# New order tables for an attention and mixture-of-experts kernel: queries before keys in the first batch, and a planner with other durations and tiling prices

## The reference

```python
n = layernorm(x)
q, k, v = split(n @ W_attn.T)                      # 16 heads of 8 channels
K, V = sums of k, v over the blocks of 4, 8, ..., 1024 tokens       # 511 "sets"
logits = concat(q @ K.T / sqrt(8), masked to sets that ended;  q . K_tail)   # tail: own, unfinished block
att = softmax(logits);  out = att @ V + att_tail * V_tail
x = x + out @ W_proj.T
h = layernorm(x); scores = sigmoid(h @ gate_w.T) + e_bias
combine = weights of the 6 best of 32 experts, within the 4 best of 8 groups
x = x + sum_e combine[e] * relu(h @ up[e].T)**2 @ down[e] + relu(h @ shared_up.T)**2 @ shared_down
```

## Time and profile before

| | |
|---|---|
| time, median of 3 runs | 617.42 us (615.31 to 617.7) |
| profiled execution | span 616.0 us; no other time is listed for it |
| TensorE busy | 556.2 us, 90% of the span |
| VectorE busy | 391.3 us, 64% |
| ScalarE busy | 371.6 us, 60% |
| GpSimd busy | 282.5 us, 46% |
| HBM traffic | 50.31 MB read, 12.06 MB written |

### The profile page before, as it was taken

The page is one execution under the profiler, slowest core; times in us unless marked ns, Lnnn a source line. Parts: engine busy times, 40 slices in busy tenths (PEclk is TensorE's granted clock), DMA queues, the critical chain, the costliest instruction groups (busy, mean ns, idle before and its releaser), DMA issues.

```text
span 616.0 us, 12273 instructions
## 1 busy us (share of the span) xinstructions
PE 556.2 (90%) x4460; PEld 358.7 (58%) x4460; DVE 391.3 (64%) x935; ACT 371.6 (60%) x536; POOL 282.5 (46%) x403
## 2 busy tenths in 40 slices
PE   7246788998899999999999999999899999999997
PEld 6033233354556555566776555666765665688896
DVE  3829967677797857847678758645678776036400
ACT  1310346773646567858655857657566769865674
POOL 2500302731735248355643547444635334366575
PEclk9755679998899999999999999899999999999999
DMA  6683000084532212775342214836322222233452
GB/s 141 181 210 82 2 4 3 14 193 153 129 88 88 75 36 78 183 209 126 90 124 66 72 35 122 190 122 141 117 74 74 79 65 67 78 118 101 124 182 92
DMA packets 49344, 63.56 MB, mean 103 GB/s; under 512 B 8484, under 2 KB 30788, under 8 KB 48004
## 3 DMA queue, kind: packets, MB, share of 16 engines
q1 hardware_dynamic: 47988, 61.60, 36.7%
q10 hardware_dynamic: 1296, 1.18, 0.6%
HBM read 50.31 MB, written 12.06 MB: 101 GB/s over the span
## 4 chain that ended last, share of the span: by engine, by line
PE 59%; DVE 23%; DMA 6%; issue 3%; ACT 3%; POOL 3%; SPq 1%; ACTq 0%; POOLq 0%; DVEq 0%
PE sums_ps L1066 16%; PE ring L1053 12%; PE sums_ps L1000 10%; DVE MXR L1173 7%; PE ring L983 4%; PE ring L961 4%; DVE XN L1121 2%; DMA QA<-q_parts 2%; PE ring L978 2%; ACT PT L824 2%; PE ring L955 2%; PE ring L1007 2%; PE ring L921 2%; PE ring L1035 1%; DMA q_parts<-Qparts 1%
## 5 line engine op out<-in xcount | busy, mean ns | idle before, releaser
L1173 DVE TENSOR_REDUCE MXR<-ring 128x4 f32<-128x1024 f32 (+2 forms) x192 | 175.3, 950 | 75.3 <-PE ring L961 73.1
L732 POOL TENSOR_TENSOR H<-RV,WB 128x512 f32<-128x512 f32 x128 | 162.3, 1279 | 121.8 <-ACT RV L835 114.4
L824 ACT ACTIVATE PT<-ring 128x1024 f32<-128x1024 f32 x160 | 158.7, 1025 | 85.5 <-PE ring L983 84.1
L1066 PE MATMUL sums_ps<-wdown,H 128*128 128x128 f32 x1152 | 155.8, 283 | 0.4 <-POOL H L732 0.3
L1066 PEld LDWEIGHTS sums_ps<-wdown,H 128*128 128x128 f32 x1152 | 141.8, 193 | 21.7 <-issue 14.7
L891 ACT ACTIVATE RV<-ring 128x512 f32<-128x512 f32 x144 | 84.9, 593 | 67.6 <-PE ring L1053 66.9
L1000 PE MATMUL sums_ps<-PT,VA 128*32 128x512 f32 (+1 forms) x768 | 88.7, 553 | 0.1
L835 ACT ACTIVATE RV<-RV 128x512 f32<-128x512 f32 x128 | 80.0, 629 | 2.6
L1053 PE MATMUL ring<-XH,WUH 128*128 128x512 f32 x144 | 67.1, 466 | 0.7 <-ACT RV L891 0.3
L961 PE MATMUL ring<-KA,QA 51*128 51x256 bf16 (+7 forms) x512 | 62.8, 311 | 0.0
L983 PE MATMUL ring<-QA,KA 54*128 54x512 bf16 (+1 forms) x384 | 60.4, 350 | 1.1 <-ACT PT L824 0.6
(11 more groups left out here) (128 smaller groups left out, 676.2 us busy)
## 6 DMA issues: line engine op xcount, KB each, us to landing
WB<-combine SPq DMA_DIRECT2D x256, 128.0 KB, 2.9
QA<-q_parts SPq DMA_DIRECT2D x16, 384.0 KB, 6.1
KA<-k_parts SPq DMA_DIRECT2D x8, 384.0 KB, 6.2
q_parts<-Qparts SPq DMA_DIRECT2D x14, 192.0 KB, 5.6
XP<-in_x_dram SPq DMA_DIRECT2D x4, 512.0 KB, 5.4
X<-in_x_dram SPq DMA_DIRECT2D x4, 512.0 KB, 4.4
out_dram<-OT SPq DMA_DIRECT2D x8, 256.0 KB, 2.3
q_parts<-Qparts SPq DMA_DIRECT2D x14, 128.0 KB, 4.8
```

Of the source, the lines that this page charges most:

```text
L732: pool.tensor_tensor(H[:, m % NHB, :], RV[:, m % NRV, :], WB[:, r % NWB, :], ALU.mult).then_inc(s_had, 1)
L824: act.activation(dst, src, ACT.Exp, scale=SCALE).then_inc(s_expa, 1)
L1066: ins = pe.matmul(dsum[:, P * i:P * i + P], H[:, m % NHB, P * i:P * i + P], wdown[:, CHUNKS[n], :], start=(n == 0 and i == 0), stop=(n == ...
L1173: ins = dve.reduce_max(MXR[:, g, i, :, q0:q0 + nq], pair("max", b, w, g, n)[:, :, at:at + ns * nq].rearrange("p e (q s) -> p e q s", s=ns) ...
```

## The change

Three things change, all in the planner; the functions that emit instructions are the same.

1. In `FILLS` q comes before k (all batches). In the first batch the q pieces of window 0 no longer wait for the key pieces, and the key pieces wait for them.
2. Durations and lags in `work()` are replaced; the lag is now that of the piece that waits, not of the one it waits for.
3. The price of a change of rows depends on the pair (`turnover`); `STAY` depends on the rows to be entered and, for `max` and `exp`, on how many pairs of banks are free. `due()` gets new constants for every kind, and further ones for the first (`FIRST`) and the last batch (`LAST`).

```diff
-FILLS = "xkqvlts"
+FILLS = "xqkvlts"
...
-LAG = {"pe": 0.24, "dve": 0.16, "act": 0.17, "pool": 0.15, "sp": 0.15}
+LAG = {"pe": 0.30, "dve": 0.13, "act": 0.14, "pool": 0.19, "sp": 0.03}
+LAG_OF = {"exp": 0.23, "max": 0.24, "pv": 0.14, "mT": 0.21, "up": 0.27, "expa": 0.20, "oevac": 0.20, "et": 0.23, "split": 0.12, "rstd2": 0.0,
+          "x1": 0.19, "sco": 0.11}
...
         for k in range(2):
-            put(("ksplit", b, k), "dve", 1.1 if k else 1.65, ("sums", b, 0), later(old("kst", b - 1), 2.0), ("ksplit", b, 0) if k else None)
+            put(("ksplit", b, k), "dve", 1.6 if k else 1.55, ("sums", b, 0), later(old("kst", b - 1), 2.0),
+                ("ksplit", b, 0) if k else None if b else ("qsplit", b, 0, 1))
         for w in range(NW):
             for k in range(2):
-                put(("qsplit", b, w, k), "dve", 1.1 if k else 1.19, ("evac", b, "q"), later(old("qst", b - 1, w), 2.0), ("ksplit", b, 1))
+                put(("qsplit", b, w, k), "dve", 1.1 if k else 1.22, ("evac", b, "q"), later(old("qst", b - 1, w), 2.0),
+                    ("ksplit", b, 1) if b or w else None)
...
-SWITCH, STAY = 0.09, 18.4
-STARTUP, PERIOD = 40.0, 101.1
-OFF = {"att0": -38.9, "att1": 44.6, "ffn0": 96.0, "ffn1": 156.6, "prep": -20.5, "post": 5.3, "max": -48.5}
-UNIT_T = 3.1
-AHEAD = {"pe": 0, "act": 0.03, "dve": 0, "pool": 0.32, "sp": 1.72}
+STAY, FEW, WAIT = {128: 33.2, 64: 18.0, 32: 26.1}, 22.5, 0.07
+def turnover(rows, kind):
+
+    to = ROWS_OF.get(kind, 128)
+    if to == rows or kind == "mT":
+        return 0.0
+    if to == 64:
+        return 0.11 if rows == 128 else 0.08
+    if to == 32:
+        return 0.165
+    return (0.14 if kind in TURNS else 0.19) - (0.02 if rows == 32 else 0.0)
+STARTUP, PERIOD = -4.5, 98.8
+OFF = {"att0": 271.7, "att1": 34.4, "ffn0": 89.4, "ffn1": 175.6, "prep": 10.9, "post": -234.0, "max": -47.2}
+UNIT_T = 4.65
+AHEAD = {"pe": 0.0, "act": 0.17, "dve": 0.0, "pool": 0.28, "sp": 2.57}
...
-    return stage_due(name) + SHIFT.get(name[0], 0.0)
+    kind, b = name[:2]
+    return stage_due(name) + SHIFT.get(kind, 0.0) + (FIRST.get(kind, 0.0) if b == 0 else LAST.get(kind, 0.0) if b == B - 1 else 0.0)
...
-            if eng == "pe" and ROWS_OF.get(kind, 128) != rows:
-                at += SWITCH
+            if eng == "pe":
+                at += turnover(rows, kind)
...
-            late = lambda x: STAY if eng == "pe" and ROWS_OF.get(x[2][0], 128) != rows else 0.0
-            pick = min((x for x in c if x[0] <= limit + (SWITCH if eng == "pe" else 0.0)), key=lambda x: (x[1] + late(x), x[0], str(x[2])))
+            if eng == "pe":
+                pairs_free = sum(all(unit is None or (FREED_BY[unit[0]],) + unit[1:] in done and done[(FREED_BY[unit[0]],) + unit[1:]] < limit + 0.3
+                                     for unit in held[j:j + 2]) for j in range(0, NBANK, 2))
+                same = lambda x: ROWS_OF.get(x[2][0], 128) == rows
+                late = lambda x: 0.0 if same(x) else STAY[ROWS_OF.get(x[2][0], 128)] + (FEW * (3 - pairs_free) if x[2][0] in ("max", "exp") else 0.0)
+                pick = min((x for x in c if x[0] <= limit + (WAIT if same(x) else 0.2)), key=lambda x: (x[1] + late(x), x[0]))
```

More of the change, by code:

```diff
@@ L146, in put @@
     def put(name, eng, us, *behind):
-        W[name] = (eng, us, [x if len(x) == 2 and isinstance(x[0], tuple) else (x, LAG[kind_engine(x[0])]) for x in behind if x])
+        lag = LAG_OF.get(name[0], LAG[eng])
+        W[name] = (eng, us, [x if len(x) == 2 and isinstance(x[0], tuple) else (x, lag) for x in behind if x])
     def later(x, us):
@@ L200, in work @@
+                    put(("red", b, w, g, n), "dve", 0.07 * len(parts) - 0.01 + 2 * cols * 1.04e-3, ("max", b, w, g, n))
+                put(("mfin", b, w, g), "dve", 0.10, ("red", b, w, g, len(MAX_UNITS[w]) - 1), ("evac", b, "l"), old("split", b - 1, w, g),
                     old("td", b - 1, w))
                 put(("split", b, w, g), "pool", 1.05, ("mfin", b, w, g), turn("mT", m - 2))
-                put(("mT", b, w, g), "pe", 0.08, ("split", b, w, g), later(turn("rows", m - 1), 1.8))
-                put(("mcopy", b, w, g), "dve", 0.14, (("mT", b, w, g), 0.25))
@@ L219, in work @@
-            put(("et", b, w), "act", 0.2, ("td", b, w), old("tailw", b - 1, w), old("den", b - 1, w))
-            put(("tailw", b, w), "pool", 1.15, ("et", b, w), ("evac", b, "t"), old("aT", b - 1, w))
-            chain = [("den", "dve", 1.25, ("ocopy", b, w, NG // 2 - 1), ("et", b, w)),
+                put(("ocopy", b, w, half), "dve", 0.4, ("oT", b, w, half))
+            put(("td", b, w), "dve", 0.19, ("mfin", b, w, NG - 1), old("et", b - 1, w))
+            put(("et", b, w), "act", 0.15, ("td", b, w), old("tailw", b - 1, w), old("den", b - 1, w))
@@ L226, in work @@
[L226 to L228 removed]
+                     ("x1", "dve", 0.6), ("stats2", "dve", 0.76), ("aggr2", "dve", 0.75),
@@ new lines, in work @@
+                     ("rstd2", "pool", 1.12), ("apply2", "dve", 1.25), ("xT", "pe", 0.44), ("xhe", "act", 0.48),
+                     ("xle", "dve", 0.6), ("logits", "pe", 1.69, ("wlow", 0)), ("sco", "act", 0.2, old("weights", b - 1, w)),
+                     ("score", "dve", 1.5), ("pairs", "dve", 2.2), ("groups", "dve", 1.2), ("groups2", "dve", 0.7, old("cT", b - 1, w)),
+                     ("experts", "dve", 1.4), ("experts2", "dve", 0.85), ("weights", "dve", 0.5), ("parts", "pool", 0.45), ("cT", "pe", 0.44),
@@ L262 @@
 ROWS_OF = {"max": 64, "exp": 64, "pv": 32}
[L263 to L268 removed]
+MAX_US = [[0.28, 0.23, 0.29], [0.25, 0.25, 0.22, 0.22, 0.20, 0.20, 0.17, 0.17]]
@@ L368, in plan @@
         start[name] = at
-        done[name] = free[eng] = at + W[name][1]
+        done[name] = free[eng] = at + W[name][1] * (2.0 if eng == "pe" and COLD[0] < at < COLD[1] else 1.0)
         heads[name[0]] += 1
```

66 lines of the change are left out of this document (33 added, 33 removed).

## The result

| | before | changed |
|---|---|---|
| median | 617.70 us (612.59 to 622.80, 15 runs) | 621.85 us (617.54 to 625.56, 15 runs) |
| profiled span | 616.0 us | 619.9 us |
| TensorE busy | 556.2 us | 557.6 us |
| ratio | | 1.0067, 95% interval 1.0045 to 1.0090 |

The change makes the kernel slower by 0.7%. The forecast was 600.5 us, its range ended at 612.

The account below looks back on a forecast made before the run. It took TensorE's own time as the bound from 181.9 to 543.3 us. Span 616.0 - 5 - 9 - 3.4 - 3 + 3.5 = 599.1 us, plus 1.4 for the median: 600.5 us, range 590 to 612.

Parts of the forecast that it names:

- First batch, -5: Stretch up to 99.6 us: earlier maxima and fewer reductions ahead of their first copy gain 5 us, bounds 2.9 and 8.
- the text's own mark (later than 47): First batch on VectorE: the prediction is wrong if reductions start later than 47 us; it expected near 46.
- Fewer changes of rows, -9: TensorE from the second x fill on: 76 fewer changes at 0.12 us each gain 9 us, lower bound 5.
- The wait for the query load, -3.4: Second batch's maxima at 140.79 us: more TensorE units as cover remove the 3.39 us wait, counted as 3.4.
- The clock, -3: TensorE from 99.6 to 181.9 us: with idle time gone, 3 us lost at the lower clock come back; may be 0.
- New waits, +3.5 for thinner covers: Ahead of `cT` and `xT`: six router chains wait about 1 us each; 3.5 us lost, bounds 0 and 20.
- Rival 4: Slower: router chain becomes the bound, five steady-part chains each wait 7.5 us, +37.5 in all, 634.5 us; chance 0.07.
- Rival 3: No effect: removed row changes hidden under other waits, start's gain given back at next chain; 616 to 618 us; chance 0.07.

Follow-up runs that it names:

- aw_bc: Changed kernel with tail-logits fill and router logits moving 128 columns, plus second to fourth expert-weight loads ahead of the query load; 613.98 us, ratio 0.9928.
- aw_red: Changed kernel with 128-column tail-logits fill and router logits, plus ready VectorE work put ahead of router steps at four places; 620.71 us, ratio 1.0035.
- aw_cover: Changed kernel with 128-column tail-logits fill and router logits, replanned with seven VectorE router durations 1.3 times as long; 617.81 us, ratio 0.9990.
- a_wide: Changed kernel with tail-logits fill and router logits moving 128 columns per matmul instead of 16 and 32; 615.52 us, ratio 0.9950.

## Why the prediction was wrong

The sum had -16.9 us for the span and came out at +3.9. By its steps the 20.8 us are: the clock 13.5 (from -3 to +10.5), the waits 9.6 (from +0.1, that is -3.4 and +3.5, to +9.7), the start and the work 2.5 the other way (-7.1 and -9.4 for -5 and -9).

- **First batch, -5: right in size, in part by luck.** The key load came at 36.50 (said: 35.9 to 37.4). The query load started at 25.75, not at the end of the key pieces. Reductions began at 47.12, not near 46, since VectorE waited for `XP` until 45.08; by the text's own mark (later than 47) this piece was wrong. The second x fill was 7.1 us earlier, not 5, but only 3.2 to 3.6 us of it by the new start; the two tests of the start alone moved the time by 3 to 4 us.
- **Fewer changes of rows, -9: right.** Like units give 9.4, the separate measurement 0.148 us a change instead of my 0.12.
- **The wait for the query load, -3.4: right in kind, and paid back beside it.** Where 3.39 us stood, the timeline of the changed kernel has 0.76:

```profile
138.32 0.23 PE L985 MATMUL ring<-KS,QS 64*128 64x128 bf16 x2 [0.76 <-issue]
```

The row names no releaser, but it is the same load: SP starts it at 131.61, its last part lands at 138.23, and TensorE goes on at 138.29. Right behind it, at 143.53, stands the new wait of 2.18 us for GpSimd's products, whose expert weights SP now loads in the main behind the query load of window 1. `aw_bc` puts three of these loads ahead, and 3.7 us of such waits go. So some 2.6 us were gained at the one load, and 3.5 us lost to products between 141 and 153 us (before: 0.3 in the whole run), which the prediction did not look at.

- **The clock, -3: wrong in sign, the first step that failed.** I saw one cause, idle time, and gave it back. The changed order puts matmuls of 16 and 32 columns side by side behind short waits, and the surplus in the low clock rose by 10.5 us. The wide units gave back 6.3 us of time. With the 3 us counted as a gain, this step is some 9 of the 21 us by the time, 13.5 by the trace.
- **New waits, +3.5 for thinner covers: far too small, the second step that failed.** Waits at full clock rose by 9.7 us, the query load's 2.6 less included. The working took the chain as 15 to 16 us long and each cover by itself, and looked for waits ahead of `cT` and `xT` only; there it was near the text (waits ahead of `cT` grew by 1.6 us). The rows of the waits show what it left out: 4.4 us more ahead of exponents, on reductions that share VectorE with the chain, and 3.5 us more ahead of down projections, on GpSimd's products. That the thin covers are the cause of the first is argued, not shown: moving four reductions ahead of router steps made it slower (`aw_red`), and more cover took some 2 to 6 us of waits away with the narrow units and made the kernel with wide units slower (`aw_cover`).
- **Rival 4** had this direction, at 37.5 us of wait; chains were nowhere late by 4.1 us. **Rival 3** came nearest in time, but by another way: the fewer changes did show, and were paid away. That TensorE idled only 7.7 of 361 us was not the safety I took it for: work taken out came back as idle time and slow clock.
- What stays open: the waits (9.7 us) and the low clock (10.5) can't be split into prices that add, since taking low clock away raised the waits (`a_wide`, `aw_cover`); what causes the new waits ahead of exponents, and the 4 us that show as no idle time; and by which way the one-input steps gained with wide units and not surely without.

## What to carry to other kernels

When a planner's prices are made finer, check the durations of the engine that shares a stretch as well: seven router durations gave back 7.4 us here, against 9.4 of work saved by all fewer changes of rows, but with wide units the same durations cost 2.3 us, so try such an edit in the kernel that will be used. Read the granted clock of each stretch beside its idle time, above all where narrow matmuls come together behind waits; work saved in front of a wait is not time saved. Test each part of a change alone: its start order, put into the kernel before, was a gain of 0.65% that the rest of the change had hidden.

## What the runs showed that I had not expected

- The clock fell to 0.50 for 10.2 us with TensorE busy 10.07 of 10.20 us, behind a stretch busy 9.66 of 10.50 at 1.00. TensorE idled 0.13 and 0.84 us of them; with 128 columns instead of 16 and 32 both long falls are gone (`a_wide`).
- Taking away 12.5 us of surplus in the low clock moved the time by 6.3 us, and over the executions of the changed kernel each us at the lower level goes with 0.26 us of time.
- A reduction over two values (one input) took 220 ns in all 8 cases, 7 of them beside a GpSimd product; an operation of the same output size with two inputs 191 to 1190 ns.
